# Two-layer relational GNN: edges ordered by relation and source, the relation's weights picked by a register, and two gathered rows per node

## What is computed

```python
def rgcn_gate_layer(x, row, col, edge_type, basis, att, gate_w, root, bias):
    w = jnp.einsum('rb,bio->rio', att, basis)          # 2 relations from 30 bases, 512 x 512
    x_j = x[col]
    msgs = []
    for r in range(NUM_RELATIONS):                     # 2
        gate = jax.nn.sigmoid(x_j @ gate_w[r, :, 0])
        msgs.append(gate[:, None] * x_j @ w[r])
    msg = jnp.where((edge_type == 0)[:, None], msgs[0], msgs[1])
    agg = jax.ops.segment_sum(msg, row, num_segments=x.shape[0])
    return agg + x @ root + bias
```

## Time and profile before

| | us |
|---|---|
| median of 3 runs | 4816.99 |
| lowest and highest run | 4809.58, 4818.27 |
| the profiled execution, span from first to last instruction | 4817.3 |

### The profile page before, as it was taken

The page is one execution under the profiler, slowest core; times in us unless marked ns, Lnnn a source line. Parts: engine busy times, 40 slices in busy tenths (PEclk is TensorE's granted clock), DMA queues, the critical chain, the costliest instruction groups (busy, mean ns, idle before and its releaser), DMA issues. The chain is left out here.

```text
span 4817.3 us, 67883 instructions
## 1 busy us (share of the span) xinstructions
PE 4301.3 (89%) x23889; PEld 3503.1 (73%) x23889; DVE 2880.3 (60%) x6014; ACT 2053.7 (43%) x3499; POOL 1203.6 (25%) x1230
## 2 busy tenths in 40 slices
PE   7879999999998954877999999999899999999967
PEld 3438878788786843653998858988499884898844
DVE  5547744377586766765785445544455444556888
ACT  1212213222243621436556753357533675334557
POOL 2431112211242002775440033300333003330010
PEclk9989999999999966888999999999999998999965
DMA  9982248622698933987442365523655236554677
GB/s 344 398 300 85 76 163 275 226 72 75 216 404 320 336 125 80 171 150 228 149 156 88 114 208 165 161 85 114 212 167 164 80 114 202 166 160 130 186 193 214
DMA packets 454415, 875.59 MB, mean 182 GB/s; under 512 B 69280, under 2 KB 109840, under 8 KB 453357
## 3 DMA queue, kind: packets, MB, share of 16 engines
q1 hardware_dynamic: 304985, 528.81, 32.5%
q0 software_dynamic: 77312, 227.96, 17.2%
q10 hardware_dynamic: 71848, 115.30, 6.8%
HBM read 567.94 MB, written 302.99 MB: 181 GB/s over the span
## 5 line engine op out<-in xcount | busy, mean ns | idle before, releaser
L1990 POOL DMA_INDIRECT hidden_agg<-edge_sums,edge_where x316 | 354.7, 1122 | 698.5 <-DVE layer_raw_inner L2077 286.2
L732 PE MATMUL hidden_O<-hidden_xh,layer_hi_inner 128*128 128x256 f32 (+1 forms) x1280 | 367.6, 287 | 0.0
L734 PE MATMUL hidden_O<-hidden_xl,layer_hi_inner 128*128 128x256 f32 (+1 forms) x1280 | 361.7, 283 | 0.0
L733 PE MATMUL hidden_O<-hidden_xh,layer_lo_inner 128*128 128x256 f32 (+1 forms) x1280 | 360.9, 282 | 0.0
L1835 POOL DMA_INDIRECT message_x<-g,edge_partner x120 | 116.4, 970 | 780.0 <-POOLq L147 458.3
L2034 ACT ACTIVATE hT_inner<-hidden_O,hidden_b 128x256 f32<-128x256 f32 (+1 forms) x320 | 123.9, 470 | 332.8 <-PE hidden_O L734 332.8
L732 PE MATMUL relation_B<-relation_weights,relation_pth 128*128 128x512 f32 x640 | 254.1, 397 | 0.0
L732 PE MATMUL root_O<-root_hi,root_xh 128*128 128x512 f32 (+1 forms) x632 | 253.9, 402 | 0.0
L733 PE MATMUL relation_B<-relation_weights,relation_ptl 128*128 128x512 f32 x640 | 253.8, 397 | 0.0
L734 PE MATMUL relation_B<-relation_weights,relation_pth 128*128 128x512 f32 x640 | 253.7, 396 | 0.0
L732 PE MATMUL output_O<-layer_hi_inner,output_hh 128*128 128x512 f32 (+1 forms) x632 | 250.2, 396 | 0.0
(11 more groups left out here) (478 smaller groups left out, 12925.0 us busy)
## 6 DMA issues: line engine op xcount, KB each, us to landing
edge_sums<-message_res SPq DMA_DIRECT2D x160, 256.0 KB
layer_raw_inner<-g SPq DMA_DIRECT2D x78, 512.0 KB, 4.0
g<-layer_raw_inner SPq DMA_DIRECT2D x78, 512.0 KB
room<-in_L_gnn_basis SPq DMA_DIRECT2D x30, 1280.0 KB
order_basis<-in_L_gnn_basis SPq DMA_DIRECT2D x18, 1280.0 KB
edge_sums<-relation_res SPq DMA_DIRECT2D x80, 256.0 KB
order_x<-in_x SPq DMA_DIRECT2D x39, 512.0 KB
normed<-order_y ACTq DMA_DIRECT2D x39, 512.0 KB
```

The costliest lines, as they stand in the source:

```text
L732: eng.matmul(out, a_hi, b_hi, start=start, stop=False)
L733: eng.matmul(out, a_lo, b_hi, start=False, stop=False)
L734: return eng.matmul(out, a_hi, b_lo, start=False, stop=stop)
L1990: eng.indirect_dma_start(agg[j % R][0:n, :], None, ed.sums[1], bass.IndirectOffsetOnAxis(ap=ed.where[1][0:n, c:c + 1], axis=0)).then_inc(g ...
```

## The change

Key 0 becomes the pair of relation and source: all edges of relation 0 stand first, sorted by source, padded to a full tile; those of relation 1 follow in the next tile. So there are 41 tiles (ET0), and every tile has one relation. How many tiles the first relation takes is computed on the chip; DVE and PE read it into a register.

- front: the one-hot matrix of key 0's low part is 256 columns wide (one half for each relation), histogram, counts and lookups have three segments instead of two, a few small steps compute where relation 1 begins, the table of key 0 is first filled with -1 (absent), and the broadcast of key 0 is made from a row that DVE has computed: ACT's queue writes it to DRAM and reads it back.
- relation: one gate vector and one set of weights a tile, at an address that holds a register; the gate multiplies the gathered row instead of the selection matrix, whose 0/1 entries need no low part; `sums` is 4 x 2 matmuls, still of 256 columns (half of them zeros), `product` is 4 x 3; only 128 x 512 are copied and split; POOL takes its index straight from the table; the hardware loop is written out; the split of the root weights moves into the loop.
- root: a node's sum is now two rows, one for each relation, so each group has two more gathers and one more addition. A node without edges of relation 0 points at the row with the bias, one without edges of relation 1 at a row of zeros.

```diff
 # front, DVE
-                        for hot, part_, w in ((hot_hi, 0, HI), (hot_lo, 1, P)):
-                            m = eng.tensor_tensor(hot[k][:, ts, :], cst.iota[:, 0:w].unsqueeze(1).to_broadcast([P, ET // 2, w]),
...
+                    for hot, w, at in ((hot_hi[0][:, ts, :], HI, hl[:, 0, 0, ts]), (hot_lo[0][:, ts, 0:P], P, hl[:, 0, 1, ts]),
+                                       (hot_lo[0][:, ts, P:2 * P], P, lo_next[:, ts]),
+                                       (hot_hi[1][:, ts, :], HI, hl[:, 1, 0, ts]), (hot_lo[1][:, ts, :], P, hl[:, 1, 1, ts])):
...
+                eng.tensor_scalar(up_i[:, :], o_ps[:, SEGS:SEGS + 1], float(P - 1), None, ALU.add).then_inc(s["base"], 1)
...
+                eng.tensor_scalar(ed.first_tiles[:, :], up_i[:, :], 7, None, ALU.logical_shift_right).then_inc(s["first"], 1)
...
 # front, ACT, ahead of its loop
+                eng.wait_ge(s["hilo"], 4)
+                eng.dma_start(ed.joint_row.rearrange("(p t) -> p t", t=ET), joint[:, :]).then_inc(s["joint"], 16)
+                eng.wait_ge(s["joint"], 16)
+                eng.dma_start(row_i[0][:, :], ed.joint_row.partition_broadcast(P)).then_inc(s["rows"], 16)
+                eng.wait_ge(s["fill"], 16)
...
 # relation, DVE
+                first = eng.value_load(ed.first_tiles[0:1, 0:1], min_val=0, max_val=ET0)
...
-                    for r in range(RELATIONS):
-                        m = eng.scalar_tensor_tensor(junk[q][:, r, :], x[q][:, :], 1.0, gw[:, r, :], ALU.mult, ALU.mult,
-                                                     accum_out=z[q][:, r:r + 1])
...
+                    at = eng.snap(relation_of(first, t) * D)
+                    eng.scalar_tensor_tensor(junk[t % 2][:, :], x[q][:, :], 1.0, gw[:, bass.ds(at, D)], ALU.mult, ALU.mult,
+                                             accum_out=z[q][:, :]).then_inc(s["z"], 1)
...
-                    eng.tensor_tensor(xl[q][:, :], x[q][:, :], xh[q][:, :].bitcast(F32), ALU.subtract).then_inc(s["lo"], 1)
...
+                    eng.scalar_tensor_tensor(xl[q][:, :], x[q][:, :], sig[q][:, :], xh[q][:, :].bitcast(F32),
+                                             ALU.mult, ALU.subtract).then_inc(s["lo"], 1)
...
+                    eng.tensor_scalar(sel[q][:, 0, :], krow[:, t * P:(t + 1) * P], ed.key[0][:, t:t + 1], None, ALU.is_equal).then_inc(s["sel"], 1)
...
-                    wait(eng, st[q], h * 48)
-                    eng.tensor_tensor(res[q][:, :], B[q % 2][:, :], bt[:, :], ALU.add).then_inc(s["res"], 1)
+                    wait(eng, st[q], t // W * 32)
+                    eng.scalar_tensor_tensor(res[q][:, :], bt[:, :], ed.in_first[:, t:t + 1], B[t % 2][:, :],
+                                             ALU.mult, ALU.add).then_inc(s["res"], 1)
...
-                run(eng, (0, index), (1, gates), (2, select), (3, low), (4, result))
-                split.low(eng)
+                static_pipeline([(4, result), (1, low_rows), (1, select), (2, low), (0, gates), (0, root_low)], ET0)
...
 # relation, ACT
-                run(eng, (1, copy), (3, high))
-                split.high(eng)
+                static_pipeline([(1, copy), (2, high), (0, gate), (0, root_high)], ET0)
...
 # relation, PE
-                        m = three(eng, A[q % 2][:, c, :, :], xh[q][:, cs], xl[q][:, cs], sh[q][:, :, :], sl[q][:, :, :], True, True)
+                        eng.matmul(A[t % 2][:, c, :, :], xh[q][:, cs], sel[q][:, :, :], start=True, stop=False)
+                        m = eng.matmul(A[t % 2][:, c, :, :], xl[q][:, cs], sel[q][:, :, :], start=False, stop=True)
...
+                    at = eng.snap(relation_of(first, t) * (KC * D))
...
-                    for r in range(RELATIONS):
-                        for c in range(KC):
-                            m = three(eng, B[q % 2][:, :], pth[q % 2][:, c, r, :], ptl[q % 2][:, c, r, :], weights[:, r * KC + c, :],
...
+                    for c in range(KC):
+                        m = three(eng, B[t % 2][:, :], pth[t % 2][:, c, :], ptl[t % 2][:, c, :], weights_of(0, c)[:, bass.ds(at, D)],
+                                  weights_of(1, c)[:, bass.ds(at, D)], c == 0, c == KC - 1)
...
 # root, POOL
-                                               bass.IndirectOffsetOnAxis(ap=ed.where[0][0:n, j:j + 1], axis=0)).then_inc(ga[q][t], 16)
+                                               bass.IndirectOffsetOnAxis(ap=ed.where[0][0:n, j:j + 1], axis=0)).then_inc(ga[q], 16)
+                    wait(eng, s["yb"], g - R + 1)
+                    for t, n in tiles_of(last(g)):
+                        j = g * TILES + t
+                        eng.indirect_dma_start(add[q][0:n, t, :], None, ed.sums[0],
+                                               bass.IndirectOffsetOnAxis(ap=ed.where_next[0:n, j:j + 1], axis=0)).then_inc(gb[q], 16)
...
 # root, DVE
+                    eng.tensor_tensor(part(y[q], o), part(O[g % 2], o), part(agg[p], o), ALU.add).then_inc(s["ya"], 1)
+                    eng.wait_ge(gb[p], landed(g))
+                    eng.wait_ge(s["ya"], g + 1)
+                    eng.tensor_tensor(part(y[q], o), part(y[q], o), part(add[p], o), ALU.add).then_inc(s["yb"], 1)
```

More of the change, by code:

```diff
@@ L23 @@
 EP = ET * P
+ET0 = ET + 1
+EP0 = ET0 * P
+FAR = 1 << 14
 EPS = 1e-5
@@ L382, in _ @@
                     basis(i)
-                for k in range(KEYS):
-                    eng.dma_start(row_i[k][:, 0:E], key_in[k].partition_broadcast(P)).then_inc(s["rows"], 16)
-                eng.dma_start(ed.sums[1][ZERO_ROW:SUM_ROWS, :], zeros).then_inc(s["zdone"], 16)
+                eng.dma_start(row_i[1][:, 0:E], dst.partition_broadcast(P)).then_inc(s["rows"], 16)
+                eng.dma_start(ed.table[0].rearrange("(t p) c -> t p c", p=P), nothing).then_inc(s["fill"], 16)
+                eng.dma_start(ed.sums[1][ZERO_ROW[1]:SUM_ROWS[1], :], zeros).then_inc(s["zdone"], 16)
+                eng.dma_start(ed.sums[0][NO_NEXT:NO_NEXT + 1, :], zeros).then_inc(s["zdone"], 16)
                 for i in range(UNITS, RING):
@@ L620, in _ @@
                 eng.wait_ge(s["scan"], 1)
-                for k in range(KEYS):
-                    m = eng.matmul(o_ps[:, k:k + 1], cst.after[0:HI, 0:HI], incl[:, k, P - 1:P], start=True, stop=True)
+                for k in range(SEGS):
+                    eng.matmul(o_ps[0:HI, k:k + 1], cst.after[0:HI, 0:HI], incl[:, k, P - 1:P], start=True, stop=True)
+                m = eng.matmul(o_ps[:, SEGS:SEGS + 1], ones[:, :], incl[:, 0, P - 1:P], start=True, stop=True)
                 m.then_inc(s["off"], 1)
@@ L865, in low, with result @@
+                def low(t):
                     eng.wait_ge(s["pth"], t + 1)
[L866 removed]
+                    wait(eng, s["B"], t - 1)
+                    eng.tensor_tensor(ptl[t % 2][:, :, :], A[t % 2][:, :, 0, :], pth[t % 2][:, :, :].bitcast(F32),
                                       ALU.subtract).then_inc(s["ptl"], 1)
[L869 to L870 removed]
+                def result(t):
+                    q = t % W
+                    if t == 0:
@@ L896, in _, with root_high @@
-                run(eng, (1, copy), (3, high))
-                split.high(eng)
+                    eng.activation(pth[t % 2][:, :, :], A[t % 2][:, :, 0, :], ACT.Copy).then_inc(s["pth"], 1)
+                def root_high(t):
+                    if t == SPLIT_AT:
+                        split.high(eng)
+                static_pipeline([(1, copy), (2, high), (0, gate), (0, root_high)], ET0)
             @block.tensor
             def _(eng):
-                def sums(t, h, q, last):
+                first = eng.value_load(ed.first_tiles[0:1, 0:1], min_val=0, max_val=ET0)
```

391 lines of the change are left out of this document (205 added, 186 removed).

## The result

| | us |
|---|---|
| before, median of 4 runs | 4813.28 |
| after, median of 4 runs (4599.99 to 4616.07) | 4609.57 |
| ratio, 95% interval | 0.959 [0.9565, 0.9615] |
| the profiled execution after, its span | 4604.1 |

A forecast was written before the change was run, and what follows sets the result against it. PE was taken to bound the relation loops and first root phase, transfers the second root phase and front. -254 + 51 + 2 + 10 = -191 us against 4817.3 gave 4626 us, range 4575 to 4705 (own range 4600 to 4650).

The forecast's parts named there:

- case A: Whole kernel: the forecast itself, 4626 us, own range 4600 to 4650, chance 0.56.
- Relation phases, -127 each: Both relation loops, bound by PE: a tile falls from 7.01 to 3.74 us, 41 tiles, 127 us less each.
- 5.2 us of filling: Relation loop: 285.6 us today against 280.4 for 40 tiles; the difference was kept, new loop 158.7 us.
- the schedule: Relation tile: DVE 2.8 us, ACT 0.63 + 0.6 + 0.2, POOL 1.25, all below PE's 3.74 us.
- Registers at 0: Relation matmuls and DVE operands: register addresses cost 0; 0.06 us on each product matmul would make 59 us.
- Root 2, +51: Second root phase, bound by transfers: a sixth stream, 122.9 MB at 404 GB/s, takes 304.2 instead of 253.5 us.
- the +90 by that rule: Second root phase: by the Trainium skill's 358 GB/s limit 367 us, total 4665; given no chance of its own.
- Root 1, +2: First root phase: PE stays the bound, only the last addition and its wait show, +2 us, up to +15.
- Rival C: Root phases: added gathers run at 186 GB/s, 78% of rows being the same; 59 + 15 us more, 4700; chance 0.12.
- Front, +10: Front: one-hots +5.5, histogram +1.6, steps to the offsets +1.6, closing steps +1; delay before the loop is lost, +10 us.
- the DVE work of 0.35 us a turn: Front loop: DVE's extra work, 14 us together, is hidden; bare it would make the front +24.
- What follows, 0: Stages after the five touched ones: nothing there is edited, so no change in time.

The follow-up runs named there:

- fixed_relation: Kernel after, with relation 0's weights and gate vector at a fixed address in the relation phases, no register read: 4608.07 us.
- skip_next: Kernel after, with the second gather skipping nodes without edges of relation 1 by a bound, over a tile ScalarE prefilled with zeros; addition kept: 4592.84 us.
- plain_row: Kernel after, with the second gather of the root phases replaced by a plain load of 256 consecutive rows of x from SP's queue: 4632.42 us.
- before_two: Kernel before, with a second gather at the same index as the first and a second addition in its root phases: 4901.29 us.
- same_row: Kernel after, with one constant changed so that absent nodes of the second gather point at the bias row too: 4734.77 us.

## Why the prediction was right, and where it was off

4626 us were forecast and 4609.57 measured; case A came in, within its own range of 4600 to 4650. The profiled execution after lies 22 us below the forecast. About half of that, 10.5 us, is variation of the unchanged rest; the changed stages gave -203 against -191, where misses of -7, -3 and -6 us (root 2, root 1, both relation phases) outweigh +5 in the front.

- **Relation phases, -127 each.** Right: -129.4 and -130.8. A tile is 3.70 us instead of 3.74 (1.6 us a phase). I kept 5.2 us of filling: the loop now runs from the first `sums` at 384.61 to the last result at 538.16, 153.6 us for 41 x 3.70 = 151.7, so 1.9. The tail from the last result to the border is 11.7 us instead of 9.3. DVE, ACT and POOL stayed below PE as the schedule said.
- **Registers at 0.** Right: fixed_relation's phases lie within 1 us.
- **Root 2, +51.** Right in mechanism (the transfers bound it, a group took 7.8 us, PE at 85%), 2 to 7 us too much. In the profiled execution the 122.9 MB flowed at 407 instead of 404 GB/s (302 instead of 304 us), and start and end cost 19.6 instead of the 24.1 us that I carried over. That the stream and not the addition is paid, skip_next shows. The 358 GB/s that the Trainium skill ("DMA: Bandwidth & Descriptors", "Where 436 GB/s comes from") gives as the limit of one core between HBM and SBUF do not hold here: 407 GB/s stood for 200 us, and the +90 by that rule is twice what was measured.
- **Root 1, +2.** -1.4, within variation. PE stayed full, but the transfers are at share 1.00 there now: plain_row (285.0), before_two and same_row show that a dearer stream comes through at once.
- **Rival C, added gathers at a slow rate.** I argued against it from today's gathers, where absent nodes share a row too. That argument was not good enough: the mechanism exists and is dear (same_row, +36 and +70 us), and the forecast held because the change points the absent nodes of the second gather at another row. The step that failed is "as today's gathers, where most nodes point at one row too, are among its 404": it took one gather's reads of the shared row for two. That the total came out right although this argument was weak is in part luck.
- **Front, +10.** Measured +14.9. Mis-sized terms: the histogram +3.3 instead of +1.6; the closing part +3.8 instead of +1, 3.2 of it the read-back of 41 rows; the one-hots and what stands ahead of them +6.6 instead of +5.5. I had priced the wider matmuls at full clock, but the histogram's granted clock is 0.72 before and 0.70 after. The steps between offsets and loop were right (+1.7, 1.6 forecast). The low part that the loop's first terms wait for came 11.6 us later (66.76 against 55.14; 9 forecast), the last scatter 11.2 us later, so the DVE work of 0.35 us a turn was hidden as said.
- **What follows, 0.** -10.5 us between the two profiles; over all kernels of the table, which don't differ there, it is 3258.6 to 3293.4, so this is no effect of the change.

## What to carry to other kernels

Cost a stage by the bound that stands in its own window: where PE was full, about half of the matmul columns took half of the time; where the transfers were full, the added stream was paid at about its bytes, as long as its filler row was its own. A gather with many absent entries is better skipped by a bound over a prefilled tile than pointed at a filler row, and if it must read fillers, each gather should have its own. A delay ahead of a loop that runs at the transfers' limit is lost nearly in full (11.6 us at the start, 11.2 at the end), so look at every one-time wait before it, also the old ones.

## What the runs showed of the hardware

- Two gathers whose absent entries read one and the same DRAM row hold the DMA engines longer than with a filler row each, even when the two rows are neighbours: 0.122 us instead of 0.098 us for a row in root 1, share 1.00 at 298 instead of 354 GB/s. Share alone doesn't show it; share with GB/s does.
- Rows skipped by the bound move no bytes: 5.2 streams at 400 GB/s in 290.9 us. The engines' time for a copied row rose a little (0.088 against 0.082 us in root 2), so a skipped row may not be quite free.
- A read of 41 rows of 2 KB (84 KB) beside one of 40 took over twice as long as two of 40 rows (5.7 against 2.5 us), and splitting it into 40 + 1 gave 2.9 us back. The rate in it was 14 to 28 GB/s for most of the time, against mostly 150 to 270 GB/s in the kernel before.
- What follows the changed stages varies with the granted clock. In skip_next the message stage (100.7 against 78.5 us) had a stretch at 0.55, mostly the lower of the two levels, 1.2 GHz. The kernel after has 1.00 in the same stretch (1998.5 to 2038.5). In the 21 us before it skip_next stood at 1.00 with PE busy 20.4 us; why the clock fell stays open:

```profile
1961.00:2001.00 40.00, 38.52 (x58) 15.64 (x56) 21.24 (x64) 20.93 (x36) 20.22 (x26) 0.55 0.58 196
```
